# Two GNN passes: edge norms spread by DMA, and the relu kept in the edge product's PSUM bank

## What is computed

```python
def _gnn_layer(edge_index, x, edge_attr, norm, We, be, Wn, bn):
    src, dst = (edge_index[0], edge_index[1])
    parts = [x[src], x[dst]]
    if edge_attr is not None:
        parts.append(edge_attr)
    e = relu(concatenate(parts, axis=-1) @ We + be)
    msg = e * norm[:, None]
    agg = segment_sum(msg, dst, num_segments=x.shape[0])
    x_new = relu(concatenate([x, agg], axis=-1) @ Wn + bn)
    return (x_new, e)
```

## Time and profile before

| | |
|---|---|
| median of 3 runs | 6016.25 us (6013.4 to 6020.16) |
| the profiled execution | 6015.73 us, span 6014.0 us |
| busy, share of the span | PE 84%, DVE 72%, POOL 59%, ACT 57% |
| memory traffic | 1274 MB, 212 GB/s over the span |
| pass 0, from its first gather to pass 1's | 3851 to 4376 us |
| pass 1 | 4376 to 4983 us |
| pass 2 | 4983 us to the end |

### The profile page before, as it was taken

How to read it: one execution, slowest core, us unless ns; L and a number is a source line. 1 busy time by engine, 2 the same in 40 slices (tenths; PEclk the granted TensorE clock), 3 DMA queues, 4 the chain that set the end, 5 groups by cost and what they waited for, 6 DMA issues and landing times. The chain is left out here.

```text
span 6014.0 us, 100399 instructions
## 1 busy us (share of the span) xinstructions
PE 5078.0 (84%) x23996; PEld 3008.8 (50%) x23996; DVE 4339.4 (72%) x11924; ACT 3405.6 (57%) x7493; POOL 3537.2 (59%) x3533
## 2 busy tenths in 40 slices
PE   4999999999994768847884888799989997777775
PEld 2666666666652235424442444466656664333332
DVE  7988888888874899958885999566645555544453
ACT  4888888888874956735663577533323333222222
POOL 3544444444421657437764775277767765777777
PEclk9999999999997977967886999899999999999998
DMA  9999997777655857736664899677667774444442
GB/s 218 308 302 299 303 299 240 244 244 238 230 189 168 290 172 214 206 118 187 203 198 128 265 294 284 204 219 218 215 210 234 234 220 146 133 130 130 132 131 80
DMA packets 909508, 1274.03 MB, mean 212 GB/s; under 512 B 248502, under 2 KB 398967, under 8 KB 902579
## 3 DMA queue, kind: packets, MB, share of 16 engines
q1 hardware_dynamic: 696170, 1063.92, 54.0%
q0 software_dynamic: 112896, 202.19, 13.9%
q10 hardware_dynamic: 100016, 3.20, 1.3%
HBM read 623.49 MB, written 654.07 MB: 212 GB/s over the span
## 5 line engine op out<-in xcount | busy, mean ns | idle before, releaser
L1738 POOL DMA_INDIRECT n_xs<-table,look x1176 | 1197.8, 1019 | 558.8 <-issue 349.8
L1439 POOL DMA_INDIRECT g_xs<-table,look x784 | 775.8, 989 | 454.1 <-issue 233.6
L1877 DVE TENSOR_TENSOR_SCAN n_dT<-n_km,n_dT,bank 128x512 f32<-128x512 uint8 x291 | 372.3, 1279 | 496.1 <-PE bank L1765 493.3
L626 POOL DMA_INDIRECT p_rows<-in_x_dram,dst_ix x392 | 390.4, 996 | 487.5 <-DMA raw_rows<-p_rows 264.7
L634 POOL DMA_INDIRECT table<-slot_pair,map_ix x392 | 397.1, 1013 | 454.5 <-ACT n_sg L742 247.7
L670 PE MATMUL bank<-n_xT,gat_w 128*128 128x512 f32 (+1 forms) x1176 | 545.2, 599 | 18.4 <-ACT n_xT L734 16.3
L689 PE MATMUL bank<-n_zT,wn 128*128 128x512 f32 (+1 forms) x1176 | 537.1, 592 | 6.6 <-ACT n_zT L734 6.6
L1750 POOL DMA_INDIRECT out_dram<-n_xn,n_row_of x392 | 385.5, 983 | 140.0 <-issue 118.5
L1557 ACT ACTIVATE g_xw<-g_xs,g_cols 128x128 f32<-128x128 f32 x1176 | 370.7, 387 | 76.1 <-PE bank L1507 49.0
L1859 ACT ACTIVATE n_xn<-bank 128x512 f32<-128x512 f32 x98 | 58.4, 596 | 624.8 <-DMA out_dram<-n_xn,n_row_of 624.8
L865 DVE COPY n_ro<-bank 128x512 f32<-128x512 f32 (+1 forms) x392 | 256.4, 685 | 197.3 <-PE bank L699 134.4
(11 more groups left out here) (278 smaller groups left out, 12574.7 us busy)
## 6 DMA issues: line engine op xcount, KB each, us to landing
table<-n_ro SPq DMA_DIRECT2D x768, 256.0 KB
g_gb<-decays SPq DMA_DIRECT2D x294, 256.0 KB
n_xd<-table SPq DMA_DIRECT2D x294, 256.0 KB
table<-g_xn SPq DMA_DIRECT2D x196, 256.0 KB
g_xo<-table SPq DMA_DIRECT2D x196, 256.0 KB
edge_feats<-n_eT SPq DMA_DIRECT2D x196, 256.0 KB
table<-n_xn SPq DMA_DIRECT2D x196, 256.0 KB
n_ea<-edge_feats SPq DMA_DIRECT2D x196, 256.0 KB
```

The lines of the kernel that those rows point to most:

```text
L626: q.indirect_dma_start(out=edge_rows[e % UX][:, u, :], out_offset=None, in_=x, in_offset=bass.IndirectOffsetOnAxis(ap=dst_ix[:, t:t + 1], ...
L1439: q.indirect_dma_start(out=xs[g % XR][:, u, :], out_offset=None, in_=tables[l], in_offset=bass.IndirectOffsetOnAxis(ap=src_ix[:, t:t + 1] ...
L1738: q.indirect_dma_start(out=xs.buffers[g % UE][:, u, :], out_offset=None, in_=tables[L], in_offset=bass.IndirectOffsetOnAxis(ap=look[:, t, ...
L1877: V.tensor_tensor_scan(in_order(dT[g][:, :]), kept(g), in_order(flat_banks[1]), 0.0 if begins(g) else carry(dT[g.before(1)]), ALU.mult, AL ...
```

## The change

In passes 0 and 1 the norms no longer pass through PE. The setup copies the f32 norms once more out of PSUM (`norm_kept`) and stores them as `norm_floats`. A new function `load_norms` on SP, one step behind `load`, broadcasts a group's 512 norms to 128 partitions, into a ring `nb` of six buffers (256 KB a group). The load of `n3` and the matmul of `weights` are gone there.

The edge product gets three banks (2, 3, 4) instead of two, and they stay in use longer. ACT runs the relu twice: once into `eT` as before (which is stored as edge features), and once from the bank back into the same bank. `messages` multiplies that bank by `nb` in place, and `totals` scans the bank. `mT` is gone. A bank is free again when the total of three groups before is made. Pass 2 stays as it was, save for line numbers and unused semaphores.

```diff
+    norm_floats = dram("norm_floats", [GE, U * P])
...
+            norm_kept = sb("norm_kept", [GE, U * P], f32, c1)
...
                     do(V.tensor_copy(norm_row[:, :], flat_banks[3][0:GE, :]))
+                    do(V.tensor_copy(norm_kept[:, :], flat_banks[3][0:GE, :]))
...
+                    sp.dma_start(norm_floats, norm_kept[:, :]).then_inc(s_st, 16)
...
+            nl_ = sems(f"n{l}_norms_loaded", UE)
...
-                n3 = ring("n3", UE, (3, P * U), bf16)
+                n3 = ring("n3", UE, (3, P * U), bf16) if last_layer else None
...
-                mT = None if last_layer else ring("mT", 2, (P, P * U))
+                nb = None if last_layer else ring("nb", UE, (P, P * U))
...
+                def edges_of(g):
+                    return flat_of(2, g) if last_layer else flat_banks[2 + g.c % 3]
+
                 def messages_of(g):
-                    return norm_of(g) if last_layer else mT[g][:, :]
+                    return norm_of(g) if last_layer else edges_of(g)
...
+                        def load_norms(g):
+                            after(sp, msg, g, UE)
+                            settle(sp)
+                            sp.dma_start(nb[g][:, :], norm_floats[ds(group(g), 1), :].broadcast_to([P, U * P]))\
+                              .then_inc(nl_[g.slot], 16)
...
-                        pipeline(sp, GE, [(2, load)] + ([(4, load_mid)] if last_layer else [(6, store_feats), (8, store_rows)]), UE)
+                        pipeline(sp, GE, [(2, load)] + ([(4, load_mid)] if last_layer else [(3, load_norms), (6, store_feats), (8, store_rows)]), UE)
...
                         def edges(g):
-                            to = flat_of(2, g)
+                            to = edges_of(g)
                             pe.wait_ge(src_c, g.count())
-                            after(pe, relu, g, 2)
+                            if last_layer:
+                                after(pe, relu, g, 2)
+                            else:
+                                after(pe, total, g, 3)
...
-                            pipeline(pe, GE, [(4, enter), (5, weights), (7, nodes), (5, edges)], UE)
+                            pipeline(pe, GE, [(4, enter), (7, nodes), (5, edges)], UE)
...
-                            after(a, msg, g, 3)
-                            S.activation(eT[g][:, :], flat_of(2, g), ACT.Relu, bias=edge_b[:, l:l + 1]).then_inc(relu, 1)
+                            if last_layer:
+                                after(a, msg, g, 3)
+                            last = S.activation(eT[g][:, :], edges_of(g), ACT.Relu, bias=edge_b[:, l:l + 1])
+                            if not last_layer:
+                                last = S.activation(edges_of(g), edges_of(g), ACT.Relu, bias=edge_b[:, l:l + 1])
+                            last.then_inc(relu, 1)
...
-                            v.wait_ge(norm, g.count())
-                            V.tensor_tensor(messages_of(g), norm_of(g), eT[g][:, :], ALU.mult).then_inc(msg, 1)
+                            if last_layer:
+                                v.wait_ge(norm, g.count())
+                            else:
+                                v.wait_ge(nl_[g.slot], g.uses())
+                            if last_layer:
+                                V.tensor_tensor(norm_of(g), norm_of(g), eT[g][:, :], ALU.mult).then_inc(msg, 1)
+                            else:
+                                V.tensor_tensor(edges_of(g), edges_of(g), nb[g][:, :], ALU.mult).then_inc(msg, 1)
```

More of the change, by code:

```diff
@@ L484, in _ @@
                     sp.dma_start(last_marks, last_mark[:, :]).then_inc(s_st, 16)
-                    sp.wait_ge(s_st, 16 * (2 * LAYERS + 8))
+                    sp.wait_ge(s_st, 16 * (2 * LAYERS + 9))
         end_phase()
@@ L1664, in net_pass @@
                 mid, oT = (ring(k, 3, (P, P * U)) if last_layer else None for k in ("midT", "oT"))
-                per_load = 16 * (3 + (not last_layer))
+                per_load = 16 * 3
                 NR = 1 if last_layer else 2
@@ L1694, in load @@
                             sp.dma_start(xd[g][:, :, :], slots_of(tables[L], g)).then_inc(ld[b], 16)
-                            sp.dma_start(n3[g][:, :], norm_rows[ds(group(g), 1), :, :].rearrange("a k e -> (a k) e"))\
-                              .then_inc(ld[b], 16)
+                            if last_layer:
+                                sp.dma_start(n3[g][:, :], norm_rows[ds(group(g), 1), :, :].rearrange("a k e -> (a k) e"))\
+                                  .then_inc(ld[b], 16)
                             sp.dma_start(km[g][:, :], keep_rows[:, ds(first_edge(g) + (0 if up else 1), P * U)]
```

## The result

The changed kernel takes 5992.18 us, median of 6 runs (5985.62 to 5996.98); the kernel before took 6018.06 beside it, median of 6 (6013.40 to 6024.45). The ratio is 0.9954, with a 95% interval of 0.9943 to 0.9965: faster, by 0.46%. The profiled execution went from 6015.7 to 5985.62 us and its span from 6014.0 to 5982.7. The forecast was 5984, with a range of 5978 to 5998.

A forecast was written before the change was run, and what follows sets the result against it. TensorE was taken to pace passes 0 and 1, with POOL 0.11 us a turn behind in pass 0. Terms -21.4 - 13.0 - 0.4 + 1.4 + 0.5 + 0.7 = -32.2 gave 5984 us, range 5978 to 5998.

The forecast's parts named there:

- The matmul's price: PE, passes 0 and 1: losing the norm matmul saves 0.22 us a turn, giving 4.89 and 5.75; bounds 0.13 and 0.31.
- Rival D: PE in pass 1: the gap at the weights goes with the matmul, 0.31 us a turn, total 5975; chance 0.04.
- Pass 1: PE-bound before and after, 98 turns each 0.22 us shorter, less 0.2 for first groups: -21.4 us (-12.8 to -30).
- Pass 0: POOL becomes the bound; gathers lose their stretches since scans read a bank, last one issued 13.0 us earlier: -13.0 us.
- The bound from pass 2 (0.958): Pass 0 gathers: at pass 2's median of 0.958 us instead of 0.944, 5.5 us would be lost, leaving -7.5.
- step 8: DMA, 276 and 287 GB/s in passes 0 and 1: nothing in steady state, +0.5 us for starting bursts and last gather's landing.
- The second relu: ACT, 0.69 us a turn, hidden until it starts some 3 us in; +0.7 us at each pass end, +1.4 in all.
- the -0.4: End of pass 0: two norm matmuls fewer after the last gather, -0.4 us.
- DVE, banks, SP: Message 0.67 and total 1.28 us unchanged, three banks freed in time, SP's later store covered: no cost.
- Setup: One more copy on DVE's path before the passes, 0.68 us: +0.7 us.
- rival B: PE idles 0.1 us a turn in pass 0 and its granted clock falls: total 6017, no change; chance 0.03.
- rival A: Pass 0: gathers stay stretched or held by something else despite the bank form, no gain there, total 5997; chance 0.08.

The follow-up runs named there:

- three_gathers: Changed kernel, but in pass 0 POOL issues three gathers a group and SP loads the fourth tile by plain DMA (wrong rows); 5970.88 us, ratio 0.9927.
- no_bias_rows: Changed kernel without the bias matmul of the node product in passes 0 and 1 (node rows lack their bias); 5931.60 us in one run.
- bias_first: Changed kernel with the node product's bias matmul moved ahead of the transposes, at the front of PE's turn; 5978.81 us, ratio 0.9935.
- the two half kernels: Norms by DMA with messages still in SBUF, 6019.43 us; the kernel before with only messages and totals scan in a PSUM bank, 6015.73 us.
- five_more_act: Changed kernel with five extra ACT copies, bank to SBUF, between the two relus of each group in passes 0 and 1; 5997.61 us in one run.
- after: The changed kernel as first measured and profiled, against the kernel before; 5992.18 us, ratio 0.9954.
- after_again: The changed kernel itself measured once more, nothing altered; 5981.61 us, ratio 0.9943 to the kernel before.
- no_norm_load: Changed kernel without the broadcast load of norms after the first six groups of passes 0 and 1 (later norms wrong); 5989.47 us, ratio 0.9956.
- after_third: The changed kernel once more, beside the version with the bias first, on the same chip; 5987.32 us, ratio 0.9952.
- the two repetitions: The unaltered changed kernel measured twice more; 5981.61 us (ratio 0.9943) and 5987.32 us (ratio 0.9952).
- the first half alone: Changed kernel with norms by DMA, but messages written to SBUF and scanned there as before; 6019.43 us, ratio 1.0007 to the kernel before.
- bank_total_only: Kernel before, norm matmul kept, with messages written to a PSUM bank and scanned there in passes 0 and 1; 6015.73 us, ratio 1.0002.

## Why the prediction was right

By its own steps:

1. **The matmul's price.** 0.22 us: exact. Turns of 4.89 (three_gathers, PE alone) and 5.75 are those worked out. Rival D is out. no_bias_rows and bias_first show where its gap belongs: to the entry and exit of the bf16 matmul that remains.
2. **Pass 1.** -21.4 forecast, -21.9 measured.
3. **Pass 0.** The last gather is issued 13.2 us earlier, forecast 13.0; one gather in 1.248 us, forecast 1.249. The bound from pass 2 (0.958) did not come: the median stayed 944. That it needs both halves was in the step's argument, and the two half kernels show it. The pass as a whole got 11.7 and not 12.7 shorter (13.0 + 0.4 - 0.7), for the landing in step 8.
4. **The second relu.** Hidden in every turn. It takes 0.65 us and not 0.69. From the last rows read to the next pass, both ends are 0.3 us longer (19.2 to 19.5, 20.9 to 21.2), which is the +0.7 and the -0.4 together. The wait at the last node product went from 0.57 to 1.14. The threshold I gave, the second relu at some 3 us of the turn, was about right: in five_more_act it starts 3.2 us into the turn (4116.24, the turn's start being 0.25 ahead of 4113.27, as in the earlier trace rows) and just begins to cost.
5. **DVE, banks, SP.** The message takes 0.674 and the scan 1.280, as the earlier trace rows had them. No wait of PE for a bank shows, and SP still waits some 1.0 us a turn (80.7 us in 78 turns, for the node product and the second relu).
6. **DMA.** 277 and 287 GB/s at 0.91 and 0.92, forecast 276 and 287. The forecast's +0.5 for bursts and landing was small: in this execution the last rows are read 5.7 us after their issue and not 4.5, +1.2; in the other two profiles +0.4 and +0.5. no_bias_rows shows how much room there was: its pass 1 moves 315 GB/s at a share of 0.96 with PE busy 400 of 400 us.
7. **Setup.** The extra copy is there; in this pair of profiles what follows comes 0.3 us later and not 0.7. In the eleven profiles with the copy SP's first input load starts at 53.31 to 54.25 us, in the two without it at 53.19 and 53.20: 0.1 to 1.1 us later, 0.5 by the median. After, and before:

```profile
53.47 1.50 SPq L598 DMA_DIRECT2D n_xm<-in_x_dram  x3
```

```profile
53.19 1.50 SPq L594 DMA_DIRECT2D n_xm<-in_x_dram  x3
```

8. **The clock.** 1.00 in both passes; rival B is out. Stretched gathers stand in the three kernels with the SBUF form (in passes 0 and 1 up to 1924, 1939 and 1934 ns), and in none of the eight with the bank form, where 963 is the longest of passes 0 and 1.

By that, the rule of the Trainium skill ("SBUF — State Buffer", "Who interferes with whom") on two SBUF inputs holds for these scans and gathers. Its inferred remark on descriptor generation, carried over to scans, does not: that belonged to rival A. The kernel before already had rows against it for tensor_tensor itself. In an earlier stage L838 adds two SBUF tiles while POOL issues the indirect DMAs of L634, which take 0.97 to 1.02 us where no L838 runs beside them (296 of them). All 50 that start at least 0.10 us into an L838 and 0.13 us or more ahead of its end take 1.04 to 1.42, as this one, which ends 0.84 us behind it:

```profile
1088.78 0.68 DVE L838 TENSOR_TENSOR n_xT<-n_xT,n_sg 128x512 f32<-128x512 f32 x1
...
1088.99 1.31 POOL L634 DMA_INDIRECT table<-slot_pair,map_ix  x1 [3.04 <-ACT n_sg L742]
```

The prediction's sentence that such a scan holds "a gather that starts inside it, until it ends" was coarse in two ways: the gather ends 0.75 us behind the scan, and one that starts in the scan's first 0.10 us is not held. Neither touched the sum, since the 13.0 us were read from the gathers themselves. One bound of the forecast was a little off: half of D's gain gives 5984 - 4.4 = 5979.6, not 5978.

What was not forecast: pass 2 took 1.7 us longer in this execution, with its code unchanged. Over the profiles it takes 1030.5 to 1034.9; the granted clock in its middle (5200 to 5800) is 0.89 in after and after_again, 0.92 before and 0.93 in no_norm_load. The length doesn't follow that clock: the longest, after_third with 1034.9, has 0.92. What sets either stays open. The median moved by 25.9 us (5992.18 from 6018.06) and the two repetitions' by 33.6 and 30.6, on either side of the 32.2 forecast; the intervals overlap, and I make nothing of the difference.

So it was right mostly for the right reasons. That the first half alone would make pass 0 slower was not among its numbers, and my own expectation for it missed by 20 us.

## What to carry to other kernels

When you shorten the engine that sets the pace, look at the engine just behind it (here 0.11 us a turn): what it loses to others begins to count at that moment, and the two fixes may each measure as nothing and work only together. Where POOL issues gathers back to back, let DVE's scans take one input from PSUM. And before taking a bf16 matmul out of an f32 chain, see whether it has a bf16 neighbour: next to one it is worth 0.22 us here, alone 0.51 (both measured with matmuls of 3 and 7 rows).

## What the runs showed of the hardware

- **A scan with two SBUF inputs holds an indirect DMA of GpSimd** that starts at least 0.10 us into it: the DMA ends 0.75 to 0.76 us behind the scan, up to 1.94 us for one of 0.94. One that starts earlier isn't held, and the scan is then up to 0.07 us longer itself (1.35 for 1.28). With one input of the scan in PSUM neither happens (after, bank_total_only). A tensor_tensor with two SBUF inputs holds them too (L838 and L634 above). The size of the loss depends on how the engines keep step: 13.0, 33.1, 12.0 us in pass 0 of three kernels.
- **A lone bf16 matmul of 7 rows among f32 ones of 128 cost 0.51 us a turn** (in one run), of which only 0.22 is what a second one beside it adds (clock 1.00). Whether the type or the few rows make the rest is not shown.
- **ACT into PSUM.** The second relu took 653 ns into its own bank, the first 687 into SBUF (mean of 78 each):

```profile
L1861 ACT ACTIVATE n_eT<-bank,edge_b 128x512 f32<-128x512 f32 x78 | 53.6, 687 | 86.9 <-PE bank L1800 86.9
L1863 ACT ACTIVATE bank<-bank,edge_b 128x512 f32<-128x512 f32 x78 | 50.9, 653 | 0.0
```

The Trainium skill, "ScalarE: Activation LUTs", section "Step-by-step: what each stage is for", calls PSUM the faster destination, and these rows point the same way. They don't separate the destination from the place, since the first relu follows idle time and the second an instruction. The same relu into the bank took 714 ns behind the copies of five_more_act, so the duration depends on what runs ahead, and the next instruction starts 0.57 or 0.58 us behind either.
